# A bias added on TensorE instead of VectorE in the expert stage of a four-layer kernel

## The reference, cut to what matters

```python
# layer 0, attention (16 heads, two kinds of weights, mixed to f), its last lines
y = f @ Wo.T + bo
mu = y.mean(axis=-1, keepdims=True)
var = jnp.mean((y - mu) ** 2, axis=-1, keepdims=True)
out = x + ln_w * (y - mu) * jax.lax.rsqrt(var + LN_EPS) + ln_b
...
# layer 0, experts: x = x + ffn(layernorm(x))
gate_logits = jax.nn.softmax(x @ gate_w + gate_b, axis=-1)
...
for e in range(E):   # 8 experts
    out = out + weights[:, e:e + 1] * (x @ expert_w[e] + expert_b[e])
```

## Time and profile before

| | us |
|---|---|
| median of 3 runs | 1927.18 |
| the 3 runs | 1924.22 to 1927.45 |
| the profiled execution, its time | 1925.72 |
| the profiled execution, its span (first to last instruction) | 1923.9 |

### The profile page before, as it was taken

The page is one execution under the profiler, slowest core; times in us unless marked ns, Lnnn a source line. Parts: engine busy times, 40 slices in busy tenths (PEclk is TensorE's granted clock), DMA queues, the critical chain, the costliest instruction groups (busy, mean ns, idle before and its releaser), DMA issues. The chain is left out here.

```text
span 1923.9 us, 26284 instructions
## 1 busy us (share of the span) xinstructions
PE 1516.7 (79%) x8359; PEld 523.8 (27%) x8489; DVE 1724.6 (90%) x3714; ACT 1578.1 (82%) x1336; POOL 1500.0 (78%) x1026
## 2 busy tenths in 40 slices
PE   3778888777788787777888888888878887788887
PEld 1122222222222222222222222222222233445657
DVE  5889999998899999988999999999999958877675
ACT  2799999999899999999999999999999951122233
POOL 3999999998999999989999999999999811001020
PEclk8799999999999999999999999999999998889898
DMA  2110000000100000001000000000000000000001
GB/s 85 47 46 14 13 13 14 17 16 7 46 13 13 16 16 14 13 12 41 17 16 13 13 13 13 14 15 17 14 13 13 7 1 1 1 1 1 1 1 44
DMA packets 32488, 33.09 MB, mean 17 GB/s; under 512 B 5657, under 2 KB 23136, under 8 KB 32352
## 3 DMA queue, kind: packets, MB, share of 16 engines
q1 hardware_dynamic: 30117, 30.12, 5.1%
q10 hardware_dynamic: 2235, 1.28, 0.2%
HBM read 22.74 MB, written 8.39 MB: 16 GB/s over the span
## 5 line engine op out<-in xcount | busy, mean ns | idle before, releaser
L1053 POOL TENSOR_TENSOR sigma_weights<-grown 128x1024 f32<-128x1024 f32 x480 | 909.0, 1897 | 0.0
L698 DVE TENSOR_SCALAR sigma_weights<-ps_sig 128x512 int32<-128x512 int32 x1024 | 691.6, 675 | 62.0 <-PE ps_sig L491 60.7
L951 ACT ACTIVATE tau_weights<-ps_tau 128x1024 f32<-128x1024 f32 x506 | 680.8, 1345 | 30.2 <-PE ps_tau L503 29.9
L937 ACT ACTIVATE sigma_weights<-sigma_weights,kernel_shape 128x2048 f32<-128x2048 f32 x256 | 595.5, 2326 | 27.4 <-POOL sigma_weights L1053 27.4
L707 DVE TENSOR_TENSOR running_max<-ps_sig,running_max 128x512 f32<-128x512 f32 x896 | 605.5, 676 | 0.0
L1026 POOL TENSOR_SCALAR grown<-sigma_weights,kernel_shape 128x1024 f32<-128x1024 f32 x480 | 539.1, 1123 | 62.6 <-DVE sigma_weights L698 62.0
L946 ACT ACTIVATE sigma_weights<-sigma_weights 128x2048 f32<-128x2048 f32 x256 | 572.6, 2237 | 0.1
L545 PE MATMUL ps_acc<-tau_weights,v_heads 128*9 128x512 f32 x2048 | 533.2, 600 | 5.1 <-DVE sums L724 2.7
L545 PE MATMUL ps_acc<-sigma_weights,v_heads 128*9 128x512 f32 x2048 | 536.1, 602 | 0.0
L491 PE MATMUL ps_sig<-q_operand,k_operand 96*128 96x512 bf16 x1024 | 401.9, 393 | 61.0 <-DVE running_max L707 35.3
L503 PE MATMUL ps_tau<-q_operand,k_operand 128*128 128x512 bf16 x885 | 278.3, 384 | 208.6 <-ACT tau_weights L951 200.4
(11 more groups left out here) (194 smaller groups left out, 1275.7 us busy)
## 6 DMA issues: line engine op xcount, KB each, us to landing
q_operand<-q_parts SPq DMA_DIRECT2D x192, 48.0 KB
k_operand<-k_parts SPq DMA_DIRECT2D x63, 144.0 KB
q_parts<-parts SPq DMA_DIRECT2D x24, 128.0 KB, 2.4
k_parts<-parts SPq DMA_DIRECT2D x18, 128.0 KB, 2.4
x_res<-in_L_attn_x SPq DMA_DIRECT2D x8, 256.0 KB, 4.3
q_operand<-max_rows SPq DMA_DIRECT2D x128, 2.0 KB
out<-x_res SPq DMA_DIRECT2D x4, 512.0 KB, 3.2
k_parts<-parts ACTq DMA_DIRECT2D x6, 128.0 KB, 2.8
```

The source lines that it names most:

```text
L698: dve.tensor_scalar(sig[:, g % SIG_RING, cols].bitcast(I32), ps_sig[:, half, :].bitcast(I32), SIGN_OFF, None, ALU.bitwise_and).then_inc(ma ...
L937: act.activation(chunk(c), chunk(c), ACT.Ln, bias=shape[:, CHUNK * c // TB % H, 1:2]).then_inc(ln_done, 1)
L951: act.activation(tau[:, g % TAU_RING, :], (ps_tau, ps_sig)[tau_bank(g)[0]][:, :, :].rearrange("p h q -> p (h q)"), ACT.Exp, scale=float(DH ...
L1053: pool.tensor_tensor(sig[:, g % SIG_RING, :], t, t, ALU.mult).then_inc(sq_ready, 1)
```

## The change

The bias is added by PE. A row of 128 ones is made in SBUF by POOL at the start of the stage. Behind each of the 8 matmuls with Wo stands a second one into the same PSUM columns, of one row (the row of ones as the stationary operand, the first row of `bo_rows` as the moving one), which accumulates. DVE's two bias additions and the tile y in SBUF are gone: `bn_stats` and the final subtract-and-multiply read `ps_my` in PSUM. DVE now waits for all eight tiles before its first `bn_stats`. PE's wait for `y_biased` ahead of the gate's matmuls becomes one for `yn_ready`, and PE waits once for the row of ones at the stage's start.

```diff
-        y = sb("y", [P, TB, D])
+        ones = sb("ones_row", [1, P])
...
                     pe.matmul(ps_y[:, t // 4, (t % 4) * P:(t % 4 + 1) * P], turned_sb[:, 0, t * P:(t + 1) * P],
-                              w["wt"][:, 3, :], start=True, stop=True).then_inc(y_ready, 1)
+                              w["wt"][:, 3, :], start=True, stop=False)
+                    pe.matmul(ps_y[:, t // 4, (t % 4) * P:(t % 4 + 1) * P], ones[:, :], w["bo"][0:1, :],
+                              start=False, stop=True).then_inc(y_ready, 1)
...
-                pe.wait_ge(y_biased, b * 2)
+                pe.wait_ge(yn_ready, b * TB + TB)
...
+            pe.wait_ge(ones_set, 1)
             rounds(pe, [(0, experts(0)), (0, biases), (0, experts(1)), (1, project), (0, experts(2)),
                         (0, experts(3)), (1, gate)], begun=True)
...
+            pool.memset(ones[:, :], 1.0).then_inc(ones_set, 1)
...
                 wait(dve, yn_ready, b * TB)
-                for g in range(2):
-                    dve.wait_ge(y_ready, b * TB + 4 * (g + 1) - FIRST)
-                    dve.tensor_tensor(y[:, 4 * g:4 * g + 4, :], ps_y[:, g, :].rearrange("p (t d) -> p t d", t=4),
-                                      four(w["bo"]), ALU.add).then_inc(y_biased, 1)
-                dve.wait_ge(y_biased, b * 2)
-                take_stats(dve, lambda t: y[:, t, :], stats[:, 0], mv[:, 0], stats_ready[0], mv_ready[0], b * TB,
+                def y(t):
+                    return ps_y[:, t // 4, (t % 4) * P:(t % 4 + 1) * P]
+
+                dve.wait_ge(y_ready, b * TB + TB - FIRST)
+                take_stats(dve, y, stats[:, 0], mv[:, 0], stats_ready[0], mv_ready[0], b * TB,
                            w["dve_passed"])
...
                 for t in range(TB):
-                    dve.tensor_scalar(yn[:, t, :], y[:, t, :], mv[:, 0, t, 0:1], rstd[:, 0, t:t + 1],
+                    dve.tensor_scalar(yn[:, t, :], y(t), mv[:, 0, t, 0:1], rstd[:, 0, t:t + 1],
                                       ALU.subtract, ALU.mult).then_inc(yn_ready, 1)
```

More of the change, by code:

```diff
@@ L1150, in mix_experts @@
         y_ready, gate_ready = sem("y_ready"), sem("gate_ready")
-        y_biased, yn_ready, z_ready = sem("y_biased"), w["yn_ready"], w["m_z_ready"]
+        yn_ready, z_ready = w["yn_ready"], w["m_z_ready"]
         stats_ready, mv_ready = (w["m_stats0"], w["m_stats1"]), (w["m_mv0"], w["m_mv1"])
@@ L1156, in mix_experts @@
         TURNED, READ, FIRST = 2 * TB, 4, TB
+        ones_set = sem("ones_set")
         bias_ready, bias_added = sem("expert_bias_ready"), sem("expert_bias_added")
```

## The result

The changed kernel takes 1942.79 us (median of 4 runs, 1941.48 to 1944.13) against 1925.70 before in the same comparison (4 runs, 1924.14 to 1927.45). The ratio is 1.0089, interval 1.0073 to 1.0105: slower, by 17.1 us, where 13.1 were worked out.

The account below looks back on a forecast made before the run. PE and DVE were taken to run side by side without slack, DVE setting the end. 3 x (4.1 + 0.15) + 0.3 = 13.1 us more gave 1939.5 us, range 1930 to 1944.

Parts of the forecast that it names:

- The direction and the place: At y in each expert-stage round: DVE has no slack there, so a later y delays the end; slower, 91% chance.
- The price of a call of other rows: In project on PE: each of the 16 calls taken at 0.42 us, since row changes cost 0.2 us each.
- the forecast's wait of 5.8 us a round: DVE ahead of the first bn_stats: wait near 5.8 us in each of three rounds, instead of 0.16.
- The first rival: In project on PE: one-row calls cost 0.22 us like any other; 4.2 us slower in all, 1930.7; chance 10%.
- The size of the delay: DVE's first bn_stats in each round: 4.1 us later, the removed 1.55 us already counted.
- The second rival: In project: half clock or dearer one-row changes, twice 0.42 for half the calls; 3.4 us more per round, 1949; chance 12%.
- DVE reading PSUM: bn_stats and last pass reading PSUM instead of SBUF: 0.15 us more per round.
- the upper bound: Last pass from PSUM at half its SBUF rate: 0.066 us more an instruction, 0.53 for eight.
- the nearer end: DVE's PSUM reads: lower bound 0, from additions at 296 and 295 ns; taken with a little, 0.15 us per round.
- The memset: Stage start: PE's first matmul waits for POOL's row of ones; 0.3 us once, between 0 and 0.8.
- What was hidden: experts(2) behind project on PE: starts later but stays hidden from DVE, with 4 us to spare.
- the last rival: DVE's waits for PE in experts(0) vanish: 1.7 us per round, 5 us; with the first rival no change; chance 4%.

## Why the prediction was right, and where a size was off

**The direction and the place.** Right: DVE had no slack at y, two instructions less on it became a wait for PE, three times a round's 1.55 us against three waits of about 7.

**The price of a call of other rows.** Right: 0.42 was taken from a 64-row call between 128-row ones, and 0.416 was measured with one row, and 6.7 us of `project` with 64 rows. That it is the change of rows and not the accumulation is shown by the 128-row and 65-row runs. With 64 rows, where the clock stays full, the forecast's wait of 5.8 us a round is there too (17.2 in three). The first rival, one-row calls at 0.22, is out.

**The size of the delay.** This term was mis-sized: 4.1 us per round stood in the sum, and (21.6 - 4.65) / 3 = 5.65 were measured. The step that failed is the one that took PE's clock as full through `project`, because it is full in the short stretch at 1586 us. The second rival, with 12%, had a clock that falls in the middle of `project`. It priced it too high, at 0.84 us a call for half of the calls. The rows show 0.72 a call, for a quarter of the calls in the first round and for somewhat under half in the second. Its reason is not borne out as it stands: PE was to be starved by the changes of shape, but the 64-row calls have the same changes and the clock stayed full. The forecast and that rival were not alternatives. Both ran, one after the other. The reading behind it, that the clock falls at 1592.8 and 1606.4 us in the kernel before, came from windows of 1 us; in windows of a quarter it falls at 1592.6 and 1606.2, which changes nothing.

**How much of it was luck.** Not the direction and not the place, but in part that the time lies inside the range. Two errors had the same sign: the lower clock added 4.9 us of waits for y, and the PSUM reads cost 1.2 us more than was said. One had the other: the waits for the experts and the expert bias, which the sum had at nothing, gave 1.4 us back, and without them the time would lie at the range's end of 1944. Where the clock was full, in the 64-row run, they gave 2.9 back, and 10.9 us were measured for the 13.1 of the sum.

**DVE reading PSUM.** Mis-sized too: 0.15 per round, measured 0.54. These are the rows of the changed kernel (busy us, mean ns):

```profile
L1286 DVE TENSOR_SCALAR y_normed<-ps_my,mv_m,rstd_m 128x128 f32<-128x128 f32 x24 | 7.9, 403 | 2.0 <-DVE mv_m L1065 1.3 <-ACT rstd_m L1073 0.7
L1061 DVE BATCH_NORM_STATS2 stats_m<-ps_my 128x6 f32<-128x128 f32 x24 | 5.1, 284 | 22.2 <-PE ps_my L1210 22.1
L1061 DVE BATCH_NORM_STATS2 stats_m<-x_res 128x6 f32<-128x128 f32 x24 | 4.9, 278 | 3.3 <-POOL x_res L1269 3.3
```

The last pass went from 342 to 403 ns, the upper bound (66 ns an instruction) nearly in full, and `bn_stats` from 278 to 284. I had taken the nearer end from a pair of two-input additions, 296 and 295 ns, and that pair could not tell: it says nothing of an instruction with one tensor input. The Trainium skill's rule that I weighed ("VectorE: DVE Perf Modes", The TRN2 errata), 62 cycles more for any VectorE instruction from PSUM, would fit the last pass alone but fails at `bn_stats` (6 ns). The Trainium skill has the one that fits in the same page, "VectorE: DVE Perf Modes", The perf-mode tier table: a float32 `tensor_scalar` runs at twice the rate from SBUF and at the single one with a PSUM operand. The 61 ns agree with it, against the 66 of the upper bound.

**The memset.** 0.3 us were taken. From the start of DVE's last instruction of the stage before to PE's first there are 0.75 us (1573.21 to 1573.96), and 0.55 before (1572.10 to 1572.65): 0.2, once and ahead of the stage.

**What was hidden.** experts(2) stayed hidden: though PE ran it partly at the lower clock, DVE's first addition of it started without a wait. The waits elsewhere gave 1.4 us back, which stands in the last rival as a mechanism, far below its 5 us.

## What to carry to other kernels

On TensorE a small call is not cheap because it is small. Ask first which class of rows its neighbours have: a call of 128 columns with 1, 32, 33 or 64 rows between 128-row calls cost 0.42 us here at the full clock, one of 65 or of 128 rows 0.22. If a bias must go through PE, give it the rows of its neighbours or put it in one call per bank ahead of them (1.0016 and 0.9996 here, for 1.0089).

Moving work from the engine that sets the end to one that is level with it gained nothing here, even with the bias left out: look at the wait at the point of transfer (0.16 us here), not at busy shares. And when an operand moves to PSUM, look for a pair of rows with the same number of tensor inputs before pricing the read.

## What the runs showed of the hardware that was not expected

- The border lies between 64 and 65 rows: 17.2 against 8.5 us of DVE's waiting, with nothing else changed.
- At the same spacing of calls, the granted clock fell from 2.4 to 1.2 GHz inside `project` with 1, 32 and 33 rows in each of nine rounds, and in none of three with 64. Between one row and 64 it came to 6.5 us of stage, of 17. Why the rows matter for the clock stays open.
- Filling 1 us of PE's gap ahead of experts(0) with work that had to be done anyway went with 4 us less of stage and of time, more than any form of the change under study gave.
